# The unit of tables 8 and 9, and the Gram of tiles 0 and 1, one place later in a recommendation tower's first stage

## What is computed

```
e = stack([tbl_f[ids[:, f]] for f in range(26)], axis=1)
combined = concatenate([e, r_dense_x[:, None, :]], axis=1)
z = einsum('bfd,bgd->bfg', combined, combined)[:, triu_i, triu_j]
h = concatenate([z, r_dense_x], axis=1)
h = maximum(h @ W_top1 + b_top1, 0)
h = maximum(h @ W_top2 + b_top2, 0)
y = h @ W_top3
```

## Time and profile before

| | |
|---|---|
| time, median of 3 runs | 361.75 us (360.04 to 362.33) |
| the profiled execution's own time | 362.72 us |
| its span, first to last instruction | 360.9 us |
| TensorE's matmuls busy | 335.2 us (93% of the span) |
| VectorE, ScalarE, GpSimd busy | 229.0, 155.2, 247.5 us |
| mean granted TensorE clock | 0.986 of full speed |

### The profile page before, as it was taken

The page is one execution under the profiler, slowest core; times in us unless marked ns, Lnnn a source line. Parts: engine busy times, 40 slices in busy tenths (PEclk is TensorE's granted clock), DMA queues, the critical chain, the costliest instruction groups (busy, mean ns, idle before and its releaser), DMA issues.

```text
span 360.9 us, 9694 instructions
## 1 busy us (share of the span) xinstructions
PE 335.2 (93%) x4080; PEld 315.3 (87%) x4080; DVE 229.0 (63%) x351; ACT 155.2 (43%) x271; POOL 247.5 (69%) x263
## 2 busy tenths in 40 slices
PE   0878889899999999999999999999999999889996
PEld 0768789899899989999899999999899999778885
DVE  5999794695267957689277957689286956101010
ACT  5779936487363223332333223332233323342432
POOL 4777777777777777777777777777777777773000
PEclk9989969999999999999999999999999999999999
DMA  7999212584243433434143433434143413343020
GB/s 187 251 245 238 60 53 61 155 270 141 56 138 95 126 87 104 121 108 117 53 123 102 129 95 102 119 111 117 53 128 96 125 53 101 90 123 97 14 70 5
DMA packets 31474, 40.76 MB, mean 113 GB/s; under 512 B 16864, under 2 KB 23984, under 8 KB 31431
## 3 DMA queue, kind: packets, MB, share of 16 engines
q1 hardware_dynamic: 22835, 22.97, 23.8%
q0 software_dynamic: 8192, 16.79, 16.7%
q10 hardware_dynamic: 403, 0.38, 0.4%
HBM read 32.75 MB, written 7.36 MB: 111 GB/s over the span
## 4 chain that ended last, share of the span: by engine, by line
PE 81%; DMA 6%; POOL 5%; ACT 4%; issue 3%; SPq 1%; ACTq 0%; DVE 0%
PE ps_o L738 36%; PE ps_g L783 15%; PE ps_l L807 10%; PE ps_t L768 7%; PE ps_l L833 7%; POOL rows L285 5%; PE ps_l L809 3%; DMA rows<-tbl,idx 2%; DMA turn<-gram 2%; ACT emb L445 1%; DMA idx<-ids_g 1%; PE ps_l L872 1%; ACT onehot L426 1%; SPq L333 1%; ACT emb L438 1%
## 5 line engine op out<-in xcount | busy, mean ns | idle before, releaser
L285 POOL DMA_INDIRECT rows<-tbl,idx x256 | 246.7, 964 | 80.6 <-issue 76.2
L620 DVE TENSOR_SCALAR onehot<-ids_b,row_of 125x513 fp32r<-125x513 int16 x290 | 192.6, 740 | 13.6 <-PE ps_o L738 7.8
L738 PE MATMUL ps_o<-onehot,tab 125*128 125x256 f32 x1248 | 161.0, 288 | 3.4 <-issue 3.4
L738 PEld LDWEIGHTS ps_o<-onehot,tab 125*128 125x128 f32 x1248 | 154.0, 193 | 3.7 <-issue 3.6
L638 DVE COPY gram<-ps_g 128x432 f32<-128x432 f32 x32 | 19.4, 607 | 87.8 <-PE ps_g L783 81.0
L438 ACT COPY emb<-ps_o 128x512 f32<-128x512 f32 x40 | 32.0, 799 | 77.3 <-PE ps_o L738 77.3
L783 PEld LDWEIGHTS ps_g<-emb 128*54 128x54 f32 x2048 | 53.8, 130 | 9.8 <-ACT emb L445 3.2
L783 PE MATMUL ps_g<-emb 128*54 128x54 f32 x2048 | 57.6, 214 | 4.0 <-ACT emb L445 2.5
L768 PE MATMUL ps_t<-ident,rows 128*128 128x128 f32 x256 | 38.5, 279 | 5.9 <-DMA rows<-tbl,idx 5.6
L445 ACT COPY emb<-ps_t 128x512 f32<-128x512 f32 (+1 forms) x65 | 42.3, 672 | 2.2 <-PE ps_t L768 1.8
L807 PE MATMUL ps_l<-z,w_sb 117*128 117x256 f32 x168 | 41.0, 379 | 0.2 <-issue 0.2
(11 more groups left out here) (37 smaller groups left out, 82.6 us busy)
## 6 DMA issues: line engine op xcount, KB each, us to landing
turn<-gram SPq DMA_DIRECT2D x62, 91.1 KB
ids_b<-ids_oh SPq DMA_DIRECT2D x39, 129.0 KB, 3.6
stage<-tbl SPq DMA_DIRECT2D x10, 448.0 KB
rows<-tbl,idx POOLq DMA_INDIRECT x256
z<-turn SPq DMA_DIRECT2D x64, 40.5 KB
turn<-gram SPq DMA_DIRECT2D x62, 21.1 KB
xs<-x SPq DMA_DIRECT2D x8, 128.0 KB, 2.2
z<-turn SPq DMA_DIRECT2D x45, 4.5 KB
```

The costliest lines, as they stand in the source:

```text
L285: nc.gpsimd.indirect_dma_start(out=rows[m % RING][:, i, :], out_offset=None, in_=gathered[GATHERED.index(f)], in_offset=bass.IndirectOffse ...
L620: nc.vector.tensor_scalar(onehot[n % BUFS][0:OH_P, 0:FILL].rearrange("p (a b) -> p a b", a=RUNS), ids_b[0:OH_P, ids_at(t, o), :, 0:RUN], r ...
L738: last = nc.tensor.matmul(ps_o[n % 2][:, j, :], tab[0:OH_P, UNIT * o + j, part, h, :], onehot[m % BUFS][0:OH_P, STEP * j:STEP * (j + 1)], ...
```

## The change

It rewrites the hand-made order of steps 0 and 1, with the same instructions. `unit(1, 2)` and `unit(0, 4)` change places, so the first unit that needs tables 8 and 9 stands one place later; `products(0)` and `products(1)` come one unit later each. ScalarE's and VectorE's lists follow. SyncE issues two loads of ids in front of `spread(0)` instead of behind it. Apart from that, ScalarE casts table 0 in front of its two fills of the first unit.

```
-FIRST_ORDER = (..., (1, 1), (0, 3), (0, 4), (1, 2), (1, 3), (1, 4))
+FIRST_ORDER = (..., (1, 1), (0, 3), (1, 2), (0, 4), (1, 3), (1, 4))
...
 sync:
             load_x(1)
             load_ids(2, 0)
-            spread(0)
-
             load_ids(2, 1)
             load_ids(2, 2)
+            spread(0)
+
             sp.wait_ge(chunk_l, NOH)
             fetch_z(0)
             load_weights()
...
 scalar:
+            chunk(0)
             make(0, 0)
-            chunk(0)
             chunk(1)
...
             chunk(8)
-            make(0, 4)
+            make(1, 2)
             keep_unit(0, 3)
             keep_quad(1, 1)
             chunk(9)
-            make(1, 2)
-            keep_unit(0, 4)
+            make(0, 4)
+            keep_unit(1, 2)
             keep_quad(1, 2)
             make(1, 3)
-            keep_unit(1, 2)
-            keep_gram(0)
+            keep_unit(0, 4)
             keep_quad(1, 3)
             make(1, 4)
             keep_unit(1, 3)
-            keep_gram(1)
+            keep_gram(0)
             make(2, 0)
             keep_unit(1, 4)
+            keep_gram(1)
...
 vector:
+            makes_of(6, 0, 3)
             chunk(8)
-            makes_of(6, 0, 3)
+            makes_of(6, 3, DVE_FILLS)
             chunk(9)
-            makes_of(6, 3, DVE_FILLS)
             makes_of(7, 0, DVE_FILLS)
-            makes_of(8, 0, 2)
+            makes_of(8, 0, DVE_FILLS)
+            makes_of(9, 0, 4)
             keep_bank(0, 0)
-            makes_of(8, 2, 4)
+            makes_of(9, 4, DVE_FILLS)
             keep_bank(0, 2)
-            makes_of(8, 4, DVE_FILLS)
-            makes_of(9, 0, 4)
+            makes(2, 0, 4)
             keep_bank(1, 0)
-            makes_of(9, 4, DVE_FILLS)
+            makes(2, 4, FILLS)
             keep_bank(1, 2)
-            makes(2, 0, BUFS)
+            makes(2, FILLS, BUFS)
...
 tensor:
             quad(1, 1)
+            unit(1, 2)
+            quad(1, 2)
             unit(0, 4)
-            quad(1, 2)
-            unit(1, 2)
-            products(0)
             quad(1, 3)
             unit(1, 3)
+            products(0)
+            unit(1, 4)
             products(1)
-            unit(1, 4)
```

More of the change, by code:

```diff
@@ L47 @@
 RING = 8
-FIRST_ORDER = ((0, 0), (1, 0), (0, 1), (0, 2), (1, 1), (0, 3), (0, 4), (1, 2), (1, 3), (1, 4))
+FIRST_ORDER = ((0, 0), (1, 0), (0, 1), (0, 2), (1, 1), (0, 3), (1, 2), (0, 4), (1, 3), (1, 4))
 FIRST_PLACES = (2, 3, 4, 5, 0, 1, 2, 3, 4, 5)
```

## The result

The changed kernel takes 363.14 us in the median of 20 runs (360.95 to 365.06), the kernel before 360.89 us (358.6 to 363.7). The ratio is 1.0063, with a 95% interval of 1.0042 to 1.0083. In two later sets of runs it was 0.9997 (0.9964 to 1.0029) and 1.0056 (1.0021 to 1.009). So the change costs up to 0.6% and gains nothing. The profiled execution took 364.56 us, 1.84 us over that of before.

A forecast was written before the change was run, and what follows sets the result against it. TensorE, busy 93% of the span, was taken as the bound, losing some 6 us around 46.87. Of 6.0 us lead 2.9 stays, less 2.4 for the clock: 0.5 gained, 361.75 - 0.5 = 361.3 us, range 357.2 to 363.7.

The forecast's parts named there:

- The path of the first part: TensorE up to the first quad of step 1: that quad at 68.5 instead of 74.54, a lead of 6.0 us.
- What is late next: Layer 1: TensorE, ready at 81.6, waits 3.2 us for z until about 84.8 and keeps 2.9 of 6.0 us.
- So the chain moves with its start, by 2.3 us and no more: SyncE's queue: spread 1 lands 15.0 us behind spread 0, as before, so z comes only 2.3 us earlier.
- its own last sentence: Sign of error in kind: spread 1 not 15 us behind spread 0, or TensorE waiting at a new place.
- the gain of 0.5: Whole kernel: 2.9 us of lead kept at layer 1 less 2.4 us of slow clock gives 0.5 us gained.
- some 6 us around 46.87: TensorE at unit(0, 4): 3.36 us wait for table 9 plus 2.7 us of slow clock behind it, to be removed.
- The clock's price: Layer 1 on TensorE: 3.2 us of idle time costs 2.4 us of slow clock behind it, ends 0 and 2.7.
- Rival 3: SyncE's chain to z starts no earlier; layer 1 waits and pays the clock: 2.0 us slower, 363.8 us; chance 0.14.
- Rival 2: Layer 1: z is in time at 81.6, so the gain is 6.0 us, 355.8 us; chance 0.13.
- Rival 1: Layer 1: the z wait comes but the clock holds or falls only briefly; gain 2.9 us, 358.9 us; chance 0.17.
- Rival 4: unit(1, 2) waits for fills or the next quad for its gather, TensorE idles as before; about 361.8 us; chance 0.04.
- The cast of table 0: ScalarE's first cast, moved ahead of two fills: counted at 0, at most 1.04 us either way.

The follow-up runs named there:

- fillers: Changed kernel plus 44 or 21 extra identity multiplications on TensorE ahead of layer 1 of step 0: 366.63 us with 44, 361.27 us with 21.
- the last version: Changed kernel with the weights loaded ahead of the first spread in six pieces, each issued after a set number of used fills: 357.34 us, ratio 0.9897.

## Why the prediction was wrong, by its own steps

**The path of the first part** was right. Forecast and measured: products of tile 0 at 56.5 and 55.98; spread 0 issued at 60.7 and 60.15; its landing 2.4 and 2.3 us behind the last issue; `products(1)` held up by 1.0 and 0.72 us; the quad of step 1 at 68.5 and 67.70. The fills of `unit(0, 4)` were late by about 0.9 us (that unit took 4.89 us), 0.7 forecast. `unit(1, 2)`, forecast free of waits, took 4.45 us here and 4.03 to 4.46 in the others.

**What is late next** was right in kind: layer 1 waits for `z` of tile 1, and the clock falls behind the wait. Both were in the forecast, and they turn 6.8 us of lead into a loss.

**The first step that failed** is "So the chain moves with its start, by 2.3 us and no more": I took the 15.0 us from one execution for a constant. The chain moved its start by 3.0 us and its end by 0.5, since it measured 17.5 us in the profile after. The changed kernel and its near variants gave 15.3 to 17.5 in eight executions, mean 16.3. The path was the one foreseen, through SyncE's queue to `z`, and the term in it was too small by 0.3 to 2.5 us. By its own last sentence the prediction calls another distance than 15 us wrong in kind, and rightly so: its reason was that the same transfers in the same order move as a block, and they do not, even between two executions of one kernel. Beside it, from the last issue of `fetch_z(1)` at 85.35 to layer 1 it was 1.5 us, with 1.1 forecast, and the slow clock cost 9.97 - 7.08 = 2.9 us, with 2.4 forecast. Together, from the gain of 0.5: -2.5 for the chain, -0.4 for the fetch, +0.7 for the earlier landing of spread 0, -0.5 for the clock, which is 2.2 us of loss. The products behind layer 1 are 2.1 us later.

The 1.1 us also made the slack look wider than it was. I let `z` be there at 86.95, when the DMA engines were nearly quiet. With the 1.5 to 1.8 us of the other executions the 85.86 of the earlier trace rows give 87.3 to 87.7, an estimate, so layer 1, at 87.67, had 0 to 0.3 us of slack and not 0.7.

**The second step that failed** is the size of what is removed, "some 6 us around 46.87". It was read from one execution too, and a high one. The kernel before was profiled at 362.72 us, and its three runs had a median of 361.75; over 20 runs it is 360.89. In the two other profiles of this order of units, the wait and the unit behind it read:

```profile
46.79 5.56 PE L738 MATMUL ps_o<-onehot,tab 125*128 125x256 f32 x32 [3.16 <-issue]
```

```profile
47.33 5.55 PE L738 MATMUL ps_o<-onehot,tab 125*128 125x256 f32 x32 [3.16 <-issue]
```

(The first is with the weights ahead, the second with the ids ahead.) The unit takes 5.56 and 5.55 us, not the 6.82 of the earlier trace rows: the wait and its slow clock are worth some 1.5 us less there than in the profile that I read.

How much of the error each step has depends on what is compared. Between the two profiles it is the chain, as summed above. For the medians, the 268.0 us from `products(2)` to the end give an estimate: `products(2)` starts at 95.1 in a median execution of the changed kernel (363.14 - 268.0) and at 92.9 in one of the kernel before (360.89 - 268.0). The forecast was 84.8 + 7.1 + 2.4 = 94.3 against the 94.75 of the profile. So the changed kernel is 0.8 us later than forecast, and the kernel before 1.9 us earlier than the execution that I read. Of the 2.7 us between the gain forecast and the loss measured, about two thirds lie in the base. The 363.14 us lie within the range that I gave, but that is luck: the range was laid around a base of 361.75, and around 360.89 it would have ended at 362.8.

**The clock's price** was interpolated between two rows, as if it followed from the length of the wait. Ahead of the second quad of step 0 it does not. This is the row of the changed kernel with the ids behind, again, and the row of the version with the weights in pieces:

```profile
21.97 0.91 PE L768 MATMUL ps_t<-ident,rows 128*128 128x128 f32 x4 [1.80 <-DMA rows<-tbl,idx]
22.52 5.43 PE L738 MATMUL ps_o<-onehot,tab 125*128 125x256 f32 x32
```

```profile
23.44 0.66 PE L771 MATMUL ps_t<-ident,rows 128*128 128x128 f32 x4 [2.46 <-DMA rows<-tbl,idx]
23.85 4.01 PE L741 MATMUL ps_o<-onehot,tab 125*128 125x256 f32 x32
```

Behind 1.80 us of wait the unit takes 5.43 us, behind 2.46 us it takes 4.01; the granted clock behind the one is 0.50 (22.40 to 24.00 us), behind the other 1.00 (24.00 to 28.00 us). In front of layer 1 the price does rise with the wait: 1.7 us behind waits of 3.09 to 4.12 us, 2.4 to 3.1 behind 4.92 to 5.87. The 2.4 us that I took for a wait of 3.2 came out as 1.7 where the wait was 3.09. The forecast's 2.4 came near the 2.9 measured only because the wait was 5.87 us long and not 3.2.

**Rival 3**, slower by 2.0 us (363.8 us), gives the size and nearly the time, but by luck and not by its own point: spread 0 landed 3 us early and the loss came all the same. Its break-even ("from a landing at 66.5 on") leaned on the same constant. **Rival 2** (`z` in time) is false in the changed kernel, and its mechanism is what the last version makes true: with the weights out of the chain the chain is 10.2 us and TensorE keeps its lead. **Rival 1** is false in every run in which layer 1 waits 3.09 us or more without fillers. **Rival 4** is false. The cast of table 0 was worth nothing, as forecast.

The Trainium skill's rule that a wait for a DMA is paid twice (TensorE: Matmul & The Clock Gate, "HAM oscillation — how this bites in real kernels") is borne out in front of layer 1, in each of the seven executions with a bare wait there of 3.09 to 5.87 us. By its half, an estimate, 6.42 us of slow time in the changed kernel would be worth 3.2 us; the trace shows 2.9. Ahead of the second quad the trace does not always agree: the 2.46 us above are a wait for a DMA that is paid once.

## What to carry to other kernels

When a reordering lets an engine run ahead, follow the data of its next dependency that does not move with it, here a chain through one DMA queue, and ask how much slack it had before (0.7 us by my reading, 0 to 0.3 by the later runs) rather than how large the removed wait is. Bulk loads that are needed late but sit in the same queue ahead of a short, urgent transfer are moved and cut into pieces first; with that the reordered kernel was 1.0% faster, without it up to 0.6% slower. A chain through a loaded DMA queue, and the price of a wait, are ranges and not numbers: take them from several executions, of the kernel before too, before a forecast within 1% is hung on them.

## What the runs showed that I had not expected

The same chain of the same transfers took 15.3 to 17.5 us in eight executions of the changed kernel and its variants with all weights in it. In the profile after, with 17.5 us, the DMA engines were not full at its end: between 79 and 83 us their share was 0.28 to 0.32 in the windows, and yet the ids issued at 70.05 were there only at 80.24 and the spread at 82.81. That a few engines still had work while the others had none is argued from the mean share and not shown, since no view tells the engines apart. The Trainium skill (DMA: Bandwidth & Descriptors, "Why a DMA increments its semaphore by 16 and not by 1") says that a DMA issued from SyncE runs on the largest number of engines up to 16 that divides the slowest dimension of both its sides, and on the lowest-numbered ones: by that, an estimate, the spread's larger pieces, of 27 rows, would go to 9 engines, and the largest of the three weight loads, of 117 rows, to 13. No run here shows it.

A load of 1.47 MB issued at once at 46 us held up a gather of 64 KB blocks so that its quad waited 2.51 us; the same bytes in six pieces between 47.7 and 57.4 us made no quad wait. In the kernel before, the whole load at 46.71 us made none wait either.
